# A four-layer mixture model on one core: experts applied to sorted rows in DRAM instead of to every token, and the two streams moved from rounds to phases

## The reference

```python
x = x + L0_xattn(ln(x), ctx)      # causal cross attention, 16 heads of 8
x = x + L0_ffn(ln(x))             # 8 experts, 128 -> 512 -> 128, relu, top 2
x = x + L1_xattn(ln(x), ctx)      # cross attention, no mask
x = x + L1_ffn(ln(x))             # 8 experts, gelu, biases, top 2
x = x + L2_xattn(ln(x), ctx)      # self attention, cross attention, small ffn, three norms
x = x + L2_ffn(ln(x))             # 8 experts that are attentions, top 2 by a small router
x = x + L3_xattn(ln(x), ctx)      # rotated, windowed cross attention
x = x + L3_ffn(ln(x))             # 8 experts, silu(gate) * up, 256 wide, top 2
# each mixture: logits -> top 2 of 8 -> weights w_e(token), zero for six experts
out = sum(w_e[token] * expert_e(ln(x)[token]) for e in range(8))
```

## Time and profile before

| | |
|---|---|
| median of 3 runs | 4655.02 us (4654.16 to 4658.78) |
| profiled execution, its time | 4650.93 us |
| its span, first to last instruction | 4649.1 us |
| mean granted TensorE clock in it | 0.939 of 2.4 GHz |
| bytes read, written | 80.08 MB, 2.10 MB |

### The profile page before, as it was taken

How to read it: one execution, slowest core, us unless ns; L and a number is a source line. 1 busy time by engine, 2 the same in 40 slices (tenths; PEclk the granted TensorE clock), 3 DMA queues, 4 the chain that set the end, 5 groups by cost and what they waited for, 6 DMA issues and landing times.

```text
span 4649.1 us, 70663 instructions
## 1 busy us (share of the span) xinstructions
PE 4053.1 (87%) x27952; PEld 3001.5 (65%) x27952; DVE 2362.9 (51%) x8103; ACT 1646.0 (35%) x3242; POOL 269.3 (6%) x483
## 2 busy tenths in 40 slices
PE   6888899888988989889898798987989879898798
PEld 4657677475774757747577485774866648676485
DVE  3456544555445544455544555445554455544555
ACT  2343234342343423434234232342333433234232
POOL 0001000010000100001000010000100001000010
PEclk9999999999999889999999998998999989899899
DMA  3000000000000000000000000000000100000000
GB/s 121 37 37 1 1 8 37 37 1 1 8 37 37 1 1 8 37 37 1 1 8 37 37 1 2 7 37 37 1 4 4 53 22 1 2 2 37 1 1 3
DMA packets 17098, 86.70 MB, mean 19 GB/s; under 512 B 2552, under 2 KB 11136, under 8 KB 12160
## 3 DMA queue, kind: packets, MB, share of 16 engines
q1 hardware_dynamic: 16000, 80.08, 4.4%
q0 software_dynamic: 768, 2.10, 0.1%
HBM read 80.08 MB, written 2.10 MB: 18 GB/s over the span
## 4 chain that ended last, share of the span: by engine, by line
PE 75%; DVE 17%; ACT 4%; issue 2%; SPq 0%; DMA 0%; POOL 0%; DVEq 0%; ACTq 0%
PE bank L407 14%; PE bank L418 12%; PE bank L337 10%; PE bank L303 5%; PE bank L495 5%; PE bank L479 4%; PE bank L355 4%; PE bank L309 4%; PE bank L293 3%; PE bank L344 3%; PE bank L326 3%; DVE h_tok L1091 2%; PE bank L553 2%; DVE mx L1141 2%; DVE qm L1114 2%
## 5 line engine op out<-in xcount | busy, mean ns | idle before, releaser
L863 ACT ACTIVATE ex<-bank 128x512 f32<-128x512 f32 x896 | 535.1, 597 | 1269.9 <-PE bank L344 1047.1
L337 PE MATMUL bank<-qm,kz 128*128 128x512 f32 x1280 | 678.5, 612 | 8.2 <-DVE qm L1114 8.2
L1141 DVE TENSOR_REDUCE mx<-bank 128x4 bf16<-128x512 f32 x640 | 440.9, 690 | 288.8 <-PE bank L328 184.6
L1215 DVE SCALAR_TENSOR_TENSOR x_tok<-bank,wts,x_tok 128x128 f32<-128x128 f32 x736 | 224.2, 346 | 711.9 <-PE bank L418 700.3
L407 PE MATMUL bank<-hT,w 128*128 128x256 f32 x2048 | 503.0, 391 | 20.5 <-ACT hid L904 20.5
L418 PEld LDWEIGHTS bank<-w,hid 128*128 128x128 f32 x4096 | 495.5, 192 | 13.5 <-issue 0.4
L418 PE MATMUL bank<-w,hid 128*128 128x128 f32 x4096 | 496.9, 275 | 0.0
L344 PEld LDWEIGHTS bank<-identb,mx 128*128 128x128 bf16 x2560 | 196.4, 100 | 378.2 <-issue 257.4
L407 PEld LDWEIGHTS bank<-hT,w 128*128 128x128 f32 x2048 | 378.9, 195 | 77.2 <-ACT hid L904 24.8
L722 POOL TENSOR_TENSOR rstd<-vare,power 128x2 f32<-128x2 f32 x192 | 134.2, 699 | 3235.0 <-DVE vare L1085 3235.0
L495 PE MATMUL bank<-ev,ex 128*128 128x65 f32 x2048 | 269.7, 275 | 49.5 <-DVE oT L1261 49.5
(11 more groups left out here) (173 smaller groups left out, 5976.4 us busy)
## 6 DMA issues: line engine op xcount, KB each, us to landing
w<-in_w SPq DMA_DIRECT2D x32, 2048.0 KB, 12.1
wproj<-in_wproj SPq DMA_DIRECT2D x1, 3328.0 KB
x_st<-in_x SPq DMA_DIRECT2D x16, 128.0 KB, 2.1
c_st<-in_ctx SPq DMA_DIRECT2D x16, 128.0 KB, 2.3
out_x<-hh_tok POOLq DMA_DIRECT2D x16, 128.0 KB, 2.2
gate<-in_gate SPq DMA_DIRECT2D x1, 1024.0 KB, 19.0
up<-in_up SPq DMA_DIRECT2D x1, 1024.0 KB, 21.0
down<-in_down SPq DMA_DIRECT2D x1, 1024.0 KB, 22.3
```

Source lines behind the costliest of these rows:

```text
L337: nc.tensor.matmul(ps[:], kz[s][:, j, :], qm[s][:, :, seq(b)], start=True, stop=False)
L863: give(nc.scalar.activation(ex[s][:, exps % 2], ps[:].rearrange("p (i q) -> p i q", i=4), ACT.Exp, scale=SCALE), *key)
L1141: give(nc.vector.tensor_reduce(mx[s][:, b, HB * j:HB * j + HB], ps[:].rearrange("p (i k) -> p i k", i=HB), AX.X, ALU.max), *k, "s", n)
L1215: ins = nc.vector.scalar_tensor_tensor(dst[:, b, :], ps[:, seq(b)], wts[s][:, b, e:e + 1], x[:, b, :], ALU.mult, ALU.add)
```

## The change

Each stream now owns 16 sequences (`HALF`), held in SBUF throughout, as 8 pairs. It works in phases instead of rounds: attention of layer 0 for its 8 pairs, then one mixture over all of its 2048 tokens, then attention of layer 1 for 8 pairs, and so on; the third phase carries each pair through layers 2 and the attention of layer 3. Stream 1 starts 100 planned us after stream 0.

For each pair a "tail" (normed rows, router, top 2) is computed inside the next pair's attention. A product with a triangular 0/1 table counts how many rows each expert has so far and gives every token two row numbers in a DRAM table `sent` (19456 rows of 512 B, 2048 to an expert). POOL scatters the normed rows there by four indirect DMAs per pair. After the last pair, VectorE makes a plan of 39 tiles of 128 rows (`TILES`, the most that 4096 rows in 8 groups can need), with an expert and a first row each. SP reads both from the plan into registers, loads the expert's weights (512, 578 or 384 KB) and the tile's rows, and stores the answers to `answered`; four slots of weights and rows, two of answers. POOL gathers each pair's two answers per token by four indirect DMAs and VectorE adds them, weighted (`combine`). The transposed context is kept in DRAM and reloaded. ScalarE clears both DRAM tables at the start.

`pauses` says where the streams take turns in a mixture: after every second tile.

```diff
-HEAD_START = 24.0
+REGION = HALF * P
+TILES = (2 * HALF * P - NE) // P + NE
+MOE_COLS = {0: 512 + CH * P, 1: 512 + CH * P + CH + P, 3: 3 * CH3 * P}
+SLOTS = 4
+HEAD_START = 100.0
...
+def pauses(n):
+    return n % 2 == 1 or n == TILES + 1
```

TensorE, in place of the loop over experts:

```diff
+def turn_rows(t):
+    i = f"rows_in{s}_{t % SLOTS}"
+    pe.wait_ge(sem[i], w.next(i, 16))
+    ps = open_bank("g", *k, "tT", t)
+    filled(nc.tensor.transpose(ps[:, 0:P], t_rows[s][:, t % SLOTS, :], ident[:]), *k, "tT", t)
+def first(t):
+    i = f"expert_in{s}_{t % SLOTS}"
+    pe.wait_ge(sem[i], w.next(i, 16))
+    taken(*k, "tT", t)
+    ps = open_bank("s1", *k, "h", t)
+    for c in range(CH):
+        mm = nc.tensor.matmul(ps[:, chunk(c)], expert[s][:, t % SLOTS, chunk(c)],
+                              t_turned[s][:, t % 2, :], start=True, stop=True)
+    filled(mm, *k, "h", t)
+def second(t):
+    taken(*k, "h", t)
+    ps = open_bank("s2", *k, "y", t)
+    for c in range(n_hid):
+        mm = nc.tensor.matmul(ps[:, 0:P], t_hid[s][:, t % 2, chunk(c)],
+                              expert[s][:, t % SLOTS, 512 + c * P:512 + (c + 1) * P],
+                              start=c == 0, stop=c == n_hid - 1)
+    filled(mm, *k, "y", t)
+for n in range(TILES + 2):
+    if n < TILES:
+        turn_rows(n)
+    if 1 <= n <= TILES:
+        first(n - 1)
+    if n >= 2:
+        second(n - 2)
+    if pauses(n):
+        yield "tiles", 2 * (1.05 + 0.24 * n_hid), 0.3
```

SP, for one mixture:

```diff
+def load_expert(t):
+    e = sp.value_load(plan[s][0:1, 1, t:t + 1], min_val=0, max_val=(NE - 1) * P)
+    sp.dma_start(expert[s][:, t % SLOTS, 0:cols_], A[f"moe{layer}"][bass.ds(e, P), :])\
+        .then_inc(sem[f"expert_in{s}_{t % SLOTS}"], 16)
+def load_rows(t):
+    r = sp.value_load(plan[s][0:1, 0, t:t + 1], min_val=0, max_val=MOE_ROWS - P)
+    sp.dma_start(t_rows[s][:, t % SLOTS, :], sent[s][bass.ds(r, P), :])\
+        .then_inc(sem[f"rows_in{s}_{t % SLOTS}"], 16)
+def store_rows(t):
+    taken(*k, "y", t)
+    r = sp.value_load(plan[s][0:1, 0, t:t + 1], min_val=0, max_val=MOE_ROWS - P)
+    sp.dma_start(answered[s][bass.ds(r, P), :], t_out[s][:, t % 2, :])\
+        .then_inc(sem[f"rows_out{s}_{t % 2}"], 16)
...
+for n in range(TILES + 2):
+    if n >= 2:
+        store_rows(n - 2)
+    if n + 2 < TILES:
+        load_expert(n + 2)
+        load_rows(n + 2)
+    if pauses(n):
+        yield "tiles"
```

POOL's indirect DMAs, which stand between the roots of the norms, and ScalarE's clearing:

```diff
+def send(i, j):
+    if w.new(f"cleared{s}", 32):
+        pool.wait_ge(sem[f"cleared{s}"], 32)
+    if j == 0:
+        pool.wait_ge(sem[f"pos_ready{s}"], w.next(f"pos_ready{s}"))
+    nc.gpsimd.indirect_dma_start(
+        sent[s][:], bass.IndirectOffsetOnAxis(ap=pos[s][:, i, j:j + 1], axis=0),
+        tail_tok[s][:, j // 2, :], None).then_inc(sem[f"scattered{s}"], 16)
+def fetch(i, j, dst, arrived):
+    nc.gpsimd.indirect_dma_start(
+        dst[:, j // 2, j % 2, :], None, answered[s][:],
+        bass.IndirectOffsetOnAxis(ap=pos[s][:, i, j:j + 1], axis=0)).then_inc(sem[arrived], 16)
...
+for s in range(STREAMS):
+    for dst in (sent[s], answered[s]):
+        act.dma_start(dst.rearrange("(p r) f -> p (r f)", p=P).rearrange("p (k n) -> p k n", n=ZEROS),
+                      zeros[:].unsqueeze(1).to_broadcast([P, MOE_ROWS // ZEROS, ZEROS]))\
+            .then_inc(sem[f"cleared{s}"], 16)
```

VectorE's weighted addition, two per token in place of eight:

```diff
+def combine(i, src, arrived):
+    x = rows_of(i)
+    dve.wait_ge(sem[arrived], w.next(arrived, 16 * 2 * NB))
+    for j in range(2):
+        for b in range(NB):
+            ins = nc.vector.scalar_tensor_tensor(x[:, b, :], src[:, b, j, :], slot_wts[s][:, i, b, j:j + 1],
+                                                 x[:, b, :], ALU.mult, ALU.add)
```

More of the change, by code:

```diff
@@ L395, in attention @@
                     by_token(k, "out", W(value_out), attT[s], P)
[L396 to L439, removed]
@@ L604, in stream @@
+                yield from last_tail((s, PAIRS - 1, "B"))
+                yield from mixture((s, "M", 1))
+                yield "gather", 0.0, 9.0
+                for i in range(PAIRS):
+                    tail = (s, i - 1, "C") if i else None
+                    k = (s, i, "L2a")
+                    if tail is not None:
+                        tail_turn(tail)
+                    turn_normed(k)
+                    yield "turns", 0.5, 0.6
                     taken(*k, "hT")
@@ L706, in _ @@
+            follow([stream(s) for s in range(STREAMS)], order)
+            for s in range(STREAMS):
+                sp.wait_ge(sem[f"stored{s}"], 16 * PAIRS)
         @block.gpsimd
@@ L785, in stream @@
                     yield "q"
-                    yield from units_then_root(units, root)
+                    yield from units(rooted=True)
                     yield "turn"
@@ L970, in stream @@
-                    k = (s, g, "L1")
+                    yield "turns"
+                    yield from attention(k, "L0q", tail=tail)
+                yield from last_tail((s, PAIRS - 1, "A"))
+                yield from mixture((s, "M", 0))
+                yield "gather"
+                for i in range(PAIRS):
+                    tail = (s, i - 1, "B") if i else None
+                    k = (s, i, "L1")
                     keys(k, "L1k", True)
                     yield "kv"
+                    if tail is not None:
+                        evacuate(attT[s][:], *tail, "tT")
@@ new lines, in stream @@
+                    yield from attention(k, "L1q", tail=tail)
+                yield from last_tail((s, PAIRS - 1, "B"))
+                yield from mixture((s, "M", 1))
+                yield "gather"
+                for i in range(PAIRS):
+                    tail = (s, i - 1, "C") if i else None
+                    k = (s, i, "L2a")
+                    if tail is not None:
+                        evacuate(attT[s][:], *tail, "tT")
+                    evacuate(hT[s][:], *k, "hT")
+                    yield "turns"
@@ new lines, in begin_units, with attention @@
+                def begin_units():
+                    zone(0)
+                    zone(1)
+                    split(qm, qf).then_inc(sem[f"split_ready{s}"], 1)
+                def attention(k, x, bias, rot=False, tail=None):
+                    taken(*k, "q")
+                    if rot:
+                        rotate(qf)
+                        settle(nc.vector.tensor_copy(qb[s][:], qf[s][:]))
+                    begin_units()
+                    yield "q"
+                    yield from attend(k, tail)
+                    yield "unit"
+                    settle(nc.vector.tensor_tensor(x[:], x[:], row(bias), ALU.add))
+                    yield "att"
+                    ps = take(*k, "out")
+                    settle_given(nc.vector.tensor_tensor(x[:], x[:], b2(ps[:, 0:NT]), ALU.add), *k, "out")
+                    norm(x, 1)
+                    yield "out"
```

947 lines of the change are left out of this document (566 added, 381 removed).

## The result

The changed kernel takes 4674.13 us (median of 7, 4666.95 to 4676.47) against 4655.02 for the one before: ratio 1.0038, interval 1.0026 to 1.005. It was forecast at 3930. A seventh of the busy matmul time went, and nothing was gained.

The account below looks back on a forecast made before the run. The prediction took TensorE to bound the kernel: 4651 - 793 - 340 + 200 + 95 + 110 = 3923 us, with 4 for the median 3927, said as 3930; range 3550 to 4260.

Parts of the forecast that it names:

- TensorE's balance, -793 us: Matmul work: 1234 us of mixtures go, 434 of tiles and 21 of rank products come, 14 of bias products go.
- Streams out of phase, -340: Slow windows of a round: one stream's thin places meet the other's units; 340 us gained, at most 560, floor nothing.
- The loop of the tiles, +200: Mixture tile steps take 7.5 us (7.1 in layer 3) where 5.9 (5.0) would do: 200 us waiting, bounds 100 and 730.
- Clearing, +95: At the start, four DMAs of 39.8 MB hold ScalarE, and so everything: 95 us, bounds nothing and 125.
- Alone, +110: Stretches where one stream lacks its partner, at start, end and hand-overs: 110 us more, bounds 50 and 250.
- POOL at nothing: POOL's 192 scatters and 192 gathers, near the store's 0.747 us, have room between steps and cost nothing.
- slower rival: POOL's indirect DMAs bind from 5.8 us each, making the kernel slower than before; 5120 at 7 us each; chance 0.03.
- VectorE at nothing: VectorE's new additions, evictions and short plan operations cost nothing, covered by the other stream's units; 736 weighted additions go.
- SP's chain at the pace of the tiles: Rival: reads of 1.0 us make SP pace the tile steps, 395 us waiting, 75 for the clock; about 4190; chance 0.22.
- a clock under 0.9 over whole phases: Written sign of a wrong forecast: a granted clock this low would put the saved TensorE time back.

Follow-up runs that it names:

- three-expert run: The kernel before with its mixtures cut to 3 of the 8 experts, nothing else changed: 3900.78 us, ratio 0.8385.
- uncoupled kernels: The kernel before without weight reloads, layer 1's mixture using layer 0's weights; stream 1 starting 24 or 120 planned us later: 4671.46 and 4697.66 us.
- run without reads: The changed kernel with constant tile addresses, SP's register reads of the plan left out: 4452.45 us, ratio 0.9579 to the kernel before.

## Why the prediction was wrong

- **TensorE's balance, -793 us: right in what goes.** The three-expert run gives 97% of the removed pitch back as time, and a kernel with mixtures of nearly the size of the tiles' runs in 3901 us. What comes, 434 us of tiles and 21 of rank products, was not measured by itself.
- **Streams out of phase, -340: the step that failed.** I read the slow windows of the earlier trace rows as two thin places meeting, and priced their parting at up to 560 us. The uncoupled kernels show 596 and 599 us of idle time in and out of step, and out of step is 26 us slower. The prediction named VectorE's load only as an average, 51%, and took the other stream's matmuls as free to run in a thin place; it did not ask whether VectorE could feed both, and VectorE is busy there for 5.86 us of 7. In the changed kernel, starting 76 planned us earlier gains 145 us, about half of it in the mixtures: out of step was a loss.
- **The loop of the tiles, +200: right in mechanism, too small.** The register read is about 0.7 us, not 0.44; the rows land after 2.8 us, not 2.1; two tiles take 8.7 us, not 7.5. By its own step times the six stretches would be 840 us, and they are 999. TensorE waits 325 us, the clock falls in the stretches, and asking earlier for the rows gives 280 back. The bounds given were also miscounted: by the same sum, free reads leave about 50 us and not 100, and reads of 2.1 us cost about 770 and not 730; the run without reads still waits 218 us. The Trainium skill's floor of about 600 ns for a `tensor_load` (DMA: Bandwidth & Descriptors, "Latency and other measured facts") was nearer than my row, and the trace agrees with it.
- **Clearing, +95: right in mechanism.** ScalarE's first activation came 68 us late and moving the clearing gave 78.
- **Alone, +110: too small by the look of the last windows**, 58 us for eight last gathers and 159 for a tile stretch without a partner at clock 0.66, where the prediction's tiles of layer 3 are 61 us of work. Its size was not measured by itself.
- **POOL at nothing: nothing speaks against it.** An indirect DMA takes 0.98 us of POOL, far from the 5.8 us of the slower rival.
- **VectorE at nothing: not borne out.** TensorE waits 119 us for the norms of the tails alone, 303 for the three largest waits for norms where it was 249 for the transposed norms before. No run left the tails out, so their price is not shown.
- **The rivals.** SP's chain at the pace of the tiles comes nearest to what happened in the stretches: it had steps of 9.2 and 8.8 us and 395 us of waiting. (The 758 us on which it charges the clock can't be found again in its own steps, whose work is 76 x 5.9 + 38 x 5.0 = 638; that would make 64 of its 75 us.) It still kept the 340 us of the phases, and so stood at 4190; without them it would have said 4530. The phase term alone moves the forecast from 3927 to 4267, just past the range, and not to 4674: the loop, the clock and what is listed below as open had to come on top. The slower rival named the wrong engine. One sign of being wrong that was written down did come true, a clock under 0.9 over whole phases: 0.857 in the mean and 0.89 in the third phase.

A rough sum: 4651 - 769 (97% of 793) = 3882; + 78 clearing, + 280 waiting for rows and the clock that goes with it, + 145 for being out of step, start and end included = 4385. The three are not independent: together they gave 332 us and not 503, since SP's throughput stands behind the latency. So at least 290 us, and more if they overlap, were not taken apart one by one. The best kernel bounds what is left: with rows early, clearing moved, the streams in step and one read less it is still 351 us above 3882. Its joint stretches take 682 us for 434 of tile work, with 145 us of waiting for the experts' weights, its last gathers 80, and the waits for the tails' norms are its largest single wait, 163 us. How much each of these is worth in time stays open.

## What to carry to other kernels

Before pricing idle windows as something that another stream could fill, look at which engine is busy inside them: an engine at 50% on the mean can be the bound exactly there. When work moves from resident weights to tiles fetched by an index, draw the loop from "buffer free" through the issuing queue, its register reads and the landing back to the first use, and give each operand the longest lead that its own buffer allows. Here the rows could be asked for two tiles earlier for nothing, and that was worth 280 us. Then look at what waits next: the time per tile of the issuing queue was right behind. Gains of single edits against the same loop don't add. Cutting the work itself to size in the old kernel is a quick way to tell a lost gain from a gain that was never there.

## What the runs showed of the hardware

- A register read of SBUF on SP ahead of a DMA cost about 0.7 us: issues 1.11 us apart with it, 0.36 to 0.48 without.
- Large DMAs in a row held the queue that issued them: of four with 9728 KB each the first took 0.64 us on ScalarE's queue, the others 21 to 26 us. Issued from SP they held SP instead.
- 64 KB of rows took 2.8 us to land behind an expert's weights, 1.8 us as a store.
- The granted clock fell where TensorE waited for rows: 1.2 GHz for most of the last stretch, which took 159 us at a mean of 0.66 with 96 us busy. With the rows asked for earlier the same matmuls took 65 us busy of 121 at 0.97. The share of busy time is 61% in the slow one and 54% in the fast one, so it alone does not tell the clock.
